# Where layer 1's 28 matmuls are cut between five banks of layer 2: from 5, 6, 5, 6, 6 to 4, 5, 5, 5, 9

## The reference

```python
def _cin_layer(xi, x0, W, b):
    Fi, F0 = (xi.shape[1], x0.shape[1])
    Wr = W.reshape(Fi, F0, -1)
    out = jnp.einsum('nie,nje,ijo->noe', xi, x0, Wr) + b[None, :, None]
    return jax.nn.relu(out)
x0 = inputs                      # 512 samples x 48 fields x 32
xs = [x0]
for W, b in ((W1, b1), (W2, b2), (W3, b3)):   # 128 outputs each
    xs.append(_cin_layer(xs[-1], x0, W, b))
return jnp.concatenate(xs, axis=1).sum(axis=-1)
...
h = jnp.concatenate([z, dense_ctx], axis=1)
h = jnp.maximum(h @ W_top1 + b_top1, 0.0)
h = jnp.maximum(h @ W_top2 + b_top2, 0.0)
y = h @ W_top3
```

## Time and profile before

| what | value |
|---|---|
| time, median of 3 runs | 2375.55 us (2373.5 to 2376.41) |
| the profiled execution's own time | 2376.26 us |
| its span, first to last instruction | 2374.5 us |
| PE matmuls busy | 2321.0 us, 98% |
| DVE busy | 2216.4 us, 93% |
| ACT busy | 2131.4 us, 90% |
| POOL busy | 1974.2 us, 83% |
| granted TensorE clock, mean | 0.990 of 2.4 GHz |

### The profile page before, as it was taken

How to read it: one execution, slowest core, us unless ns; L and a number is a source line. 1 busy time by engine, 2 the same in 40 slices (tenths; PEclk the granted TensorE clock), 3 DMA queues, 4 the chain that set the end, 5 groups by cost and what they waited for, 6 DMA issues and landing times.

```text
span 2374.5 us, 67987 instructions
## 1 busy us (share of the span) xinstructions
PE 2321.0 (98%) x14238; PEld 1201.3 (51%) x14238; DVE 2216.4 (93%) x8837; ACT 2131.4 (90%) x7965; POOL 1974.2 (83%) x2257
## 2 busy tenths in 40 slices
PE   3899999999999999999999999999999999999999
PEld 2455555555555555555555555555555555555554
DVE  7799999999999999999999999999999999999995
ACT  3799999999999999999999999999999999999994
POOL 6698888888888888888888888888888877777773
PEclk7899999999999999999999999999999999999999
DMA  5234333343334433353333433334333343333331
GB/s 173 48 74 80 66 70 73 68 75 73 69 67 76 76 64 73 72 70 73 72 67 70 78 70 67 72 71 72 72 72 65 72 79 65 68 72 66 68 72 30
DMA packets 194313, 170.96 MB, mean 72 GB/s; under 512 B 156068, under 2 KB 159783, under 8 KB 194248
## 3 DMA queue, kind: packets, MB, share of 16 engines
q0 software_dynamic: 42864, 136.87, 31.4%
q1 hardware_dynamic: 151384, 33.50, 7.1%
HBM read 12.83 MB, written 0.00 MB: 5 GB/s over the span
## 4 chain that ended last, share of the span: by engine, by line
PE 90%; ACT 4%; POOL 3%; issue 2%; DMA 1%; DVE 1%; SPq 0%; ACTq 0%; DVEq 0%; POOLq 0%
PE y L567 78%; PE m L557 8%; PE m L539 3%; ACT work L697 2%; POOL rows_sb L343 1%; POOL zl L453 1%; DMA work<-work 0%; ACT zh L725 0%; PE y L593 0%; DMA xT<-lo 0%; DVE acc L936 0%; ACT work L727 0%; PE y L651 0%; POOL part L418 0%; PE y L585 0%
## 5 line engine op out<-in xcount | busy, mean ns | idle before, releaser
L567 PE MATMUL y<-whi,xT 128*128 128x512 f16 x6144 | 1990.2, 380 | 4.7 <-DMA xT<-lo 4.2
L697 ACT ACTIVATE work<-y,xc 128x128 f32<-128x128 f32 x5632 | 1620.8, 431 | 137.1 <-PE y L567 116.4
L936 DVE SCALAR_TENSOR_TENSOR acc<-y,xc,acc 128x128 f32<-128x128 f32 x5632 | 1618.5, 341 | 78.9 <-PE y L567 72.1
L567 PE MATMUL y<-wlo,xT 128*128 128x512 f16 x3072 | 1164.8, 379 | 0.0
L567 PEld LDWEIGHTS y<-whi,xT 128*128 128x128 f16 x6144 | 599.4, 98 | 625.6 <-ACT work L697 13.3
L567 PEld LDWEIGHTS y<-wlo,xT 128*128 128x128 f16 x3072 | 300.9, 98 | 236.1
L418 POOL TENSOR_TENSOR part<-work 128x512 f32<-128x512 f32 x255 | 323.8, 1270 | 79.5 <-DMA work<-work 56.0
L453 POOL TENSOR_TENSOR zl<-work,zh 128x1152 f16<-128x1152 f32 x128 | 343.0, 2680 | 8.3 <-ACT work L727 8.3
L391 POOL DMA_DIRECT2D work<-work x255 | 228.4, 896 | 108.4 <-ACT work L697 106.9
L343 POOL DMA_INDIRECT rows_sb<-tbl,ids_sb x192 | 204.1, 1063 | 44.4 <-issue 43.0
L727 ACT ACTIVATE work<-m 128x512 f32<-128x512 f32 (+1 forms) x384 | 224.9, 586 | 0.0
(11 more groups left out here) (120 smaller groups left out, 2093.6 us busy)
## 6 DMA issues: line engine op xcount, KB each, us to landing
work<-work POOLq DMA_DIRECT2D x255, 512.0 KB, 4.7
xT<-hi SPq DMA_TRANSPOSE x256, 4.6
xT<-lo SPq DMA_TRANSPOSE x256, 3.6
rows_sb<-tbl,ids_sb POOLq DMA_INDIRECT x192, 2.6
xx<-w SPq DMA_DIRECT2D x4, 768.0 KB, 8.5
work<-w SPq DMA_DIRECT2D x4, 768.0 KB, 14.7
emb<-rows_sb SPq DMA_DIRECT2D x28, 96.0 KB, 3.8
x0T<-x0hl SPq DMA_TRANSPOSE x128, 2.2
```

Source lines behind the costliest of these rows:

```text
L567: ins = nc.tensor.matmul(dst[:], xT[layer][:, parity, a, :], w[layer][:, cols], start=i == 0, stop=i == 2)
L697: nc.scalar.activation(prods[layer][:, a, k * P:(k + 1) * P], bank[:, k * P:(k + 1) * P], ACT.Copy, scale=xc[layer][:, parity, j:j + 1]).t ...
L936: ins = nc.vector.scalar_tensor_tensor(dst, y, col, mine, ALU.mult, ALU.add)
```

## The change

The cuts are no longer computed as 28c/5 but stand in a tuple. Before, they were 0, 5, 11, 16, 22, 28, which gives parts of 5, 6, 5, 6 and 6 matmuls. Now they are 0, 4, 9, 14, 19, 28, which gives 4, 5, 5, 5 and 9.

```diff
 KF = KT - 1                      # 9
 L1_PASSES = 3 * KF + 1           # 28
+
+L1_CUTS = (0, 4, 9, 14, 2 * KF + 1, L1_PASSES)
...
                 if c == 0:
                     wait(pe, s_zts, t * 3 + 3)
-                for i in range(L1_PASSES * c // 5, L1_PASSES * (c + 1) // 5):
+                for i in range(L1_CUTS[c], L1_CUTS[c + 1]):
                     if i == 2 * KF:
                         wait(pe, s_zst, t + 1)
                     if i == 2 * KF + 1:
```

## The result

The changed kernel takes 2377.72 us (median of 20 runs, 2375.26 to 2380.05), the one before 2374.78 us in the same comparison. The ratio is 1.0014, with an interval of 1.0008 to 1.0019: slower by 1.9 to 4.5 us, 2.9 in the middle, and within the 0.2% that the forecast called no change. The forecast was +1.6 us. The execution that was profiled took 2380.05 us, the slowest of the twenty, at a span of 2378.2 us.

A forecast was written before the change was run, and what follows sets the result against it. PE, busy for 98% of the span, was taken to bound the kernel. The terms -4.2 + 3.3 + 1.9 + 0.6 = +1.6 us on a median of 2375.55 gave 2377.2 us, range 2371.0 to 2380.0.

The forecast's parts named there:

- my sum: Likeliest case, chance 0.68: the `zl` gain less costs at banks 1 and 3, +1.6 us, median 2377.2 us.
- The `zl` waits: PE's waits for POOL's `zl` move behind bank 4 and go in the steady part: gain 4.2 us.
- The spare behind the longest wait: Bank 4 takes 0.65 us, the longest `zl` wait is 0.58, so 0.07 us is left.
- the cover of POOL's lateness: Bank 4 hides POOL's late `zl`; 0.1 us later would bring back a stub, 0.03 us seven times.
- Bank 1: Reached one short matmul earlier, so PE waits longer for ACT in every second step: 59 x 0.056 = 3.3 us.
- ACT hangs on bank 6: ACT last waited for PE behind the previous step's block, a place the change does not move; bank 1 cost paid in full.
- Bank 3: Reached two short matmuls earlier, PE waits 0.037 us for DVE's `ends` in about 50 steps, 1.9 us; six others 0.6 us.
- Nothing at banks 2 and 4: These banks come 0.11 and 0.17 us earlier; nothing waits there, and ACT and DVE cannot use the earlier banks.
- Rival A: Only the `zl` waits count, banks 1 and 3 cost nothing: 2371.3 us, chance 0.20.
- B: Margins at banks 1 and 3 are eaten, each step pays the full 0.112 us: 2385.2 us, chance 0.04.
- C: The `zl` wait only moves behind bank 4, costs at banks 1 and 3 on top: 2381.3 us, chance 0.04.
- D: Weight loads limit the part of 9, 0.098 us spacing from the seventh matmul: 2392.8 us, chance 0.04.

The follow-up runs named there:

- the first experiment: Changed kernel with cuts (0, 5, 11, 16, 19, 28), so against the kernel before only the `zl` wait moved behind bank 4: 2370.69 us against 2374.52, ratio 0.9985.
- the two second ones: Second profiles of the kernel before and the changed kernel, no edit; the changed one took 2383.81 us, a single run.
- the run of 16: Changed kernel with cuts (0, 16, 17, 18, 19, 28), 16 short matmuls ahead of bank 1: 2370.58 us, a single run.
- the last three experiments: Changed kernel without one ACT square, 2374.39 us; with DVE's stacked_lo behind bank 23's last product, 2374.31; with that move and cuts (0, 6, 11, 16, 19, 28), 2368.74.

## Why the prediction was right

The direction and the mechanism came out as forecast: my sum was the likeliest case, and the result is near it. By its own steps:

1. The `zl` waits. Forecast 4.2 us of gain, with both profiles' blocks it is 4.2, and the kernel with this part alone is 3.8 us faster. The spare behind the longest wait, forecast as 0.07 us, is 0.07 in the first experiment; in the changed kernel it is 0.135, since PE's longer stall at bank 1 comes before it. The gain was not all kept, though. In one of the seven long ones the gain was given back in the same step. The changed kernel, timeline of DVE and then of the weight loads near 2040 us:

```profile
2040.51 1.55 DVE L906 TENSOR_SCALAR mx<-mx 128x2 f32<-128x2 f32 x1
```
```profile
2042.69 0.10 PEld L569 LDWEIGHTS y<-whi,xT 128*128 128x128 f16 x1 [0.28 <-DVE acc L938]
...
2045.47 0.10 PEld L569 LDWEIGHTS y<-whi,xT 128*128 128x128 f16 x1 [0.47 <-DVE acc L938]
```

This small DVE instruction takes 0.20 us in a usual step. In the steps where `zl` is late it takes longer too: 0.91 us in most of them, 1.55 in this one. In the kernel before it took as long, in the step whose `zl` wait is the last of the earlier trace rows:

```profile
2037.44 1.56 DVE L904 TENSOR_SCALAR mx<-mx 128x2 f32<-128x2 f32 x1
```

The trace shows what it waits for. In the changed kernel POOL's timeline of the same stretch is:

```profile
2038.67 2.68 POOL L455 TENSOR_TENSOR zl<-work,zh 128x1152 f16<-128x1152 f32 x1
2041.01 1.02 POOL L409 TENSOR_TENSOR rest<-work 128x256 f32<-128x256 f32 x1
```

POOL is busy with these two until 2042.03, and the DVE instruction ends at 2040.51 + 1.55 = 2042.06. In every profile this DVE instruction takes over 0.4 us 15 or 16 times in the steady part, and each time it ends 0.03 to 0.04 us behind a POOL `TENSOR_TENSOR` that ran beside it. (In nine steps behind 1930 us it is long although `zl` is in time; there it is POOL's `rest` beside which it runs.) So the late POOL instruction can delay PE in two ways, by `zl` itself and by way of DVE. That is read from the trace; no experiment tested it.

In the kernel before, PE stood still for 0.53 us in this step because of POOL's `zl`, and that covered DVE's delay. Without the stall PE comes earlier to a bank that DVE has not emptied, and the step is as long as before: 0.48 us more behind the block than before. All kernels with the `zl` wait moved show the same loss, 0.39 to 0.64 us, and the three others with the wait in place show none. I had named the cover of POOL's lateness, but not looked at what the stall itself was covering. Why POOL is late in such steps is left open.

2. Bank 1. Forecast 59 x 0.056 = 3.3 us; 3.4 in the profiles, in 60 steps, and +3.4 alone. That ACT hangs on bank 6, behind the block, and not on a place inside it, is what made the cost of a short matmul full, and it held: ACT starts bank 6 at the same distance behind the block, 1.608 us from the start of its last matmul, in all profiles to 0.001 us. Taking an instruction from ACT removed the wait. What the stall cost before the change, 0.062 us, is one draw out of 0.03 to 0.06; that doesn't alter this term, as the added 0.056 comes on top of any wait above zero. It was luck that ACT's pace was the same in the two first profiles: between the two second ones the 124 steps differ by 8.2 us and not by 3.2.

3. Bank 3. Forecast 1.9 + 0.6 us; 3.3 in the profiles. The wait itself has the size forecast: in the start times of the changed kernel bank 3 follows its short matmul by 0.094 us instead of 0.056, 0.038 more. But the second matmul of the bank then follows by 0.226 instead of 0.216 us. So a new wait costs its length and 0.010 us on top, 0.048 a step. Bank 1 paid these 0.010 before already. 47 steps pay this, 2.3 us in all, the five with the short `zl` waits among them, which I had left out. The other 1.1 us lie in eleven steps in which DVE is later than usual; I had counted six and 0.6. This is the term that was mis-sized.

4. Nothing at banks 2 and 4: right, no wait stands there in the profile of the changed kernel, and the users of the early banks turned them into nothing.

Rival A (only the `zl` waits count, 2371.3) describes the first experiment, not the change. B did not come: the steps without the ACT wait pay 0.048 and not 0.112 us. C did not either, for PE no longer waits for `zl` in the steady part. D is excluded by the run of 16. The forecast total, +1.6, is short of the profiles' +3.2 by 0.8 at bank 3, 0.1 at bank 1 and the 0.7 lost behind two blocks. The measured times give +2.9, with an interval of 1.9 to 4.5.

## What to carry to other kernels

Work that is strewn between banks of a ring has two jobs: it gives its inputs time, and it gives the ring's readers time. A wait at the place where an input comes late is cured by moving that part behind another bank, but the matmuls must be taken from parts behind the tight banks, not from the parts ahead of them. Before moving anything, read for each bank in the stretch how far its reader's end lies before the start, less the latency; a move by more than that is paid in full in every step, and waits of 0.05 us times 100 steps outweigh seven of up to 0.6 that the list of waits shows. Ask also what a stall was covering: when it goes, the next late engine shows.

## What the runs showed of the hardware

When PE has waited, the second matmul behind the wait comes 0.226 us after the first instead of 0.216. In all profiles the weight load of a waiting matmul at bank 1 starts 0.004 us ahead of it and not 0.054. In the kernel before, with the matmuls at 1005.76 and 1023.45 (the first of them in the earlier trace rows):

```profile
1005.75 0.10 PEld L567 LDWEIGHTS y<-whi,xT 128*128 128x128 f16 x1
1023.39 0.10 PEld L567 LDWEIGHTS y<-whi,xT 128*128 128x128 f16 x1
```

So I take it that the weight loads have lost their lead; that was not tested by itself.

PE's waits in the steady part end 0.053 to 0.059 us after the releaser's last instruction, in all profiles here: 0.053 to 0.057 for ACT, 0.055 to 0.057 for POOL, 0.056 to 0.059 for DVE.

DVE's `mx` instruction (a `TENSOR_SCALAR` on 128 x 2 f32) does not end while a POOL `TENSOR_TENSOR` that was running at its start goes on, once through two of them in a row: in the kernel before and the changed one it takes 0.2 to 1.56 us and ends 0.035 to 0.039 us behind POOL in all 16 cases over 0.4 us. In the last three experiments, where it mostly starts behind POOL's instruction, it takes 0.158. DVE's products, which read a PSUM bank, take their usual 0.34 to 0.35 us beside the same POOL instruction. No experiment moved POOL's instruction to test this.

ACT's pace against PE's is not constant: 12.26 to 12.34 us for the same stretch of instructions, while PE's steps are 17.678 us in all kernels without a wait. DVE did not show this: its `ends` came 2.054 to 2.058 us behind the first matmul of the block in all profiles in which its order is the same. A margin of a few hundredths of a microsecond between ACT and PE can so be a wait in one execution and none in the next.

The spacing of short matmuls with a weight load each is 0.056 us for runs of 4, 5, 6, 9 and 16, with a granted clock that is 0.99 to 1.0 of 2.4 GHz.
